# One transformer-style layer on one core: tokens spread over the partitions by a product, setup reordered, eight products of ones on TensorE

## What is computed

```
w_emb = fake_quant(emb_weight)                 # scale = max|w| / 127, round, scale back
e = w_emb[tok]                                 # 125 x 128 table, tokens 0..124
h = relu(conv over the previous and this token, fake_quant(conv_weight))
x = layernorm(h)
Wq = w_qkv / sigma_est * sigma                 # sigma_est by one power step: v = W u, u2 = W^T v
q, k, v = split(x @ Wq.T);  dots = q k^T * exp(temperature), own position masked
h = h + softmax(dots) v @ Wo.T + b_out         # Wo scaled in the same way
h = h + experts(layernorm(h))
```

## Time and profile before

| | |
|---|---|
| median of 3 runs | 495.35 us (495.01 to 495.76) |
| profiled execution, its own time | 495.01 us |
| its span, first to last instruction | 493.2 us |
| outside the span | 1.8 us |
| TensorE busy | 472.3 us (96% of the span), 3824 instructions |
| VectorE busy | 423.6 us (86%) |
| ScalarE busy | 363.8 us (74%) |
| GpSimd busy | 300.6 us (61%) |

### The profile page before, as it was taken

How to read it: one execution, slowest core, us unless ns; L and a number is a source line. 1 busy time by engine, 2 the same in 40 slices (tenths; PEclk the granted TensorE clock), 3 DMA queues, 4 the chain that set the end, 5 groups by cost and what they waited for, 6 DMA issues and landing times.

```text
span 493.2 us, 11360 instructions
## 1 busy us (share of the span) xinstructions
PE 472.3 (96%) x3824; PEld 404.6 (82%) x3824; DVE 423.6 (86%) x722; ACT 363.8 (74%) x688; POOL 300.6 (61%) x357
## 2 busy tenths in 40 slices
PE   2989999999999999999999999999999999999897
PEld 2945788888988898888788898889888988888685
DVE  5469989988998898889998999899989999999465
ACT  1258878887788778877888688878887887683553
POOL 2114697888668866874468857885788556751000
DMA  6500009531953195362622592259225932000002
GB/s 233 218 1 0 2 15 213 127 87 36 200 116 85 34 200 120 85 131 52 126 66 68 108 202 59 73 105 204 56 72 105 202 69 64 0 2 3 3 17 73
DMA packets 29484, 44.78 MB, mean 91 GB/s; under 512 B 3200, under 2 KB 21120, under 8 KB 29184
## 3 DMA queue, kind: packets, MB, share of 16 engines
q1 hardware_dynamic: 28864, 44.21, 38.4%
q10 hardware_dynamic: 576, 0.00, 0.1%
HBM read 6.46 MB, written 1.05 MB: 15 GB/s over the span
## 4 chain that ended last, share of the span: by engine, by line
PE 81%; DVE 13%; issue 2%; DMA 2%; ACT 2%; SPq 0%; POOL 0%; DVEq 0%; ACTq 0%
PE ps L696 22%; PE ps L680 19%; PE ps L662 10%; PE ps L663 10%; PE ps L603 5%; DVE pt_lo L1361 4%; DVE neg_max L1377 4%; PE ps L739 3%; PE ps L598 2%; PE ps L887 2%; DMA arena<-in_wqkv_rows 2%; PE ps L870 2%; PE ps L573 1%; DVE x L1198 1%; PE ps L901 1%
## 5 line engine op out<-in xcount | busy, mean ns | idle before, releaser
L1361 DVE TENSOR_TENSOR pt_lo<-ps,pt_hi 128x512 fp32r<-128x512 f32 x256 | 163.5, 680 | 1.3 <-ACT pt_hi L1036 1.3
L1377 DVE TENSOR_REDUCE neg_max<-ps 128x1 f32<-128x1024 f32 x128 | 156.6, 1223 | 6.5 <-PE ps L667 2.6
L1036 ACT ACTIVATE pt_hi<-ps 128x512 fp32r<-128x512 f32 x256 | 139.3, 596 | 29.4 <-PE ps L680 29.2
L438 POOL TENSOR_SCALAR probs<-probs,inv_sum 128x1024 f32<-128x1024 f32 x128 | 144.6, 1129 | 26.6 <-POOL inv_sum L435 26.6
L696 PE MATMUL ps<-pt_hi,v_slot 128*128 128x256 f32 x512 | 150.0, 324 | 0.0
L1056 ACT ACTIVATE probs<-ps,neg_max 128x1024 f32<-128x1024 f32 x128 | 142.5, 1113 | 6.9 <-DVE neg_max L1377 4.0
L680 PE MATMUL ps<-ident,probs 128*128 128x128 f32 x1024 | 133.7, 273 | 1.5 <-DVE pt_lo L1361 0.9
L680 PEld LDWEIGHTS ps<-ident,probs 128*128 128x128 f32 x1024 | 117.6, 140 | 19.8 <-POOL probs L438 3.0
L696 PE MATMUL ps<-pt_lo,v_slot 128*128 128x256 f32 x512 | 127.8, 282 | 0.0
L435 POOL TENSOR_TENSOR inv_sum<-row_sum,powers 128x1 f32<-128x1 f32 x128 | 70.8, 553 | 83.2 <-ACT probs L1056 83.2
L696 PEld LDWEIGHTS ps<-pt_hi,v_slot 128*128 128x128 f32 x512 | 96.8, 189 | 9.7 <-issue 9.7
(11 more groups left out here) (145 smaller groups left out, 391.6 us busy)
## 6 DMA issues: line engine op xcount, KB each, us to landing
q_st<-arena SPq DMA_DIRECT2D x28, 256.0 KB, 3.8
k_hi<-arena SPq DMA_DIRECT2D x28, 256.0 KB, 5.1
k_lo<-arena SPq DMA_DIRECT2D x28, 256.0 KB, 5.2
v_slot<-v_all SPq DMA_DIRECT2D x14, 512.0 KB, 3.9
arena<-arena SPq DMA_DIRECT2D x28, 256.0 KB, 4.9
f_sb<-in_f SPq DMA_DIRECT2D x2, 1024.0 KB, 10.1
x<-in_tok SPq DMA_DIRECT2D x2, 512.0 KB, 7.6
w_slot<-in_w_pairs SPq DMA_DIRECT2D x8, 128.0 KB, 2.0
```

What stands on the lines that cost most here:

```text
L438: pool.tensor_scalar(probs[:, t % 4, :], probs[:, t % 4, :], inv_sum[:, t % 4:t % 4 + 1], 1.0, ALU.mult, ALU.mult).then_inc(norm_done, 1)
L1036: act.activation(dst, ps[:, transposes_bank(t, a, drain), :].rearrange("p (j c) -> p j c", c=P), ACT.Copy).then_inc(hi_done, 1)
L1361: dve.tensor_tensor(pt_lo[at], ps[:, transposes_bank(t, a, drain), :].rearrange("p (j c) -> p j c", c=P), pt_hi[at].bitcast(F32), ALU.subt ...
L1377: dve.tensor_reduce(neg_max[:, t % 4:t % 4 + 1], ps[:, SCORES + 2 * (t % 2):SCORES + 2 * (t % 2) + 2, :].rearrange("p a c -> p (a c)"), AX ...
```

## The change

It touches only the setup and the first step of the first pair.

- The tokens are loaded once, as 16 rows of 128 (8 KB). GpSimd caps them and converts them (`tok_f`), then `tokens_apart(b)` multiplies, for eight rows, the row by a column of `ident`, so that each of 16 partitions holds 1024 elements with its own 128 tokens at its own place and zeros elsewhere. TensorE's `spread_tokens(b)` multiplies this with a matrix of ones of 16 rows: two products of 512 columns, after which every partition of the bank holds the tokens. VectorE compares out of PSUM, in two halves.
- `conv` and the tokens are issued by ScalarE, ahead of `u_sb`; the weight rows are second in SyncE's queue.
- GpSimd makes five constants first (`ident` first of all), then does tokens and the four steps of the convolution's quantisation, then the other constants.
- TensorE runs eight products of `ones` with itself, which nobody reads, between `spread_tokens(0)` and the wait for the weight rows. The Gram matrix is cut in four products before the embedding and eight after `embed(1)`. The order is now: `top`, spread 0, ones, Gram 0 to 3, `embed(0)`, spread 1, `embed(1)`, Gram 4 to 11, `embed(2)`, `gu`, transposes.
- `v_ps` moves behind the projection `dq0`; the first head's order is `dk0`, `dq0`, `dk1`, `dq1`, in other banks; the ratio stands ahead of the first `first_low`.
- `embed(3)` moves behind the first scores, into step 0 of the first pair, with ScalarE's `embedded(3)` and then the exponential of step 0 ahead of that step's values.

```diff
-        top, gram_ps, gu_ps, sums_ps = ps[:, 2, 0:VOCAB], ps[:, 3, 0:P], ps[:, 3, 0:1], ps[:, 3, 0:2]
-        v_ps, u2_ps, out_sums_ps = ps[:, TRANS, 0:1], ps[:, PV_BANK, 0:4], ps[:, WORK, 0:2]
+        top, gram_ps, gu_ps = ps[:, 2, 0:VOCAB], ps[:, 3, 0:P], ps[:, 3, 0:1]
+        sums_ps, v_ps, u2_ps, out_sums_ps = ps[:, WORK, 0:2], ps[:, WORK, 4:5], ps[:, WORK, 8:12], ps[:, WORK, 0:2]
...
-        EMBED_BANKS = (0, 1, 2, WORK)
-        FIRST_HEAD = {"dk0": WORK, "dk1": TRANS, "dq0": 2, "dq1": TRANS + 1}
+        TOKEN_BANKS = TRANS
+        EMBED_BANKS = (0, 1, 2, TRANS)
+        FIRST_HEAD = {"dk0": 0, "dq0": 1, "dk1": 3, "dq1": TRANS + 1}
...
+            const(pool.memset(ident[:, :], 0.0))
+            pool.wait_ge(const_ready, count[0])
+            const(pool.affine_select(out=ident[:, :], in_=ident[:, :], compare_op=ALU.not_equal, fill=1.0,
+                                     base=0, pattern=[[-1, P]], channel_multiplier=1))
             const(pool.memset(ones[:, :], 1.0))
+            const(pool.memset(ones_r[:, :].bitcast(F32), 1.0))
...
+            pool.wait_ge(tok_loaded, 16)
+            pool.tensor_scalar(tok_f[:, :], tok_sb[:, :], float(VOCAB - 1), 1.0, ALU.min, ALU.mult).then_inc(tok_ready, 1)
+            pool.wait_ge(const_ready, 2)
+            pool.wait_ge(tok_ready, 1)
+            def tokens_apart(b):
+
+                pool.tensor_tensor(tok_diag[:, b, :, :], tok_f[:, :].unsqueeze(1).broadcast_to([TILES, NT, P]),
+                                   ident[0:TILES, NT * b:NT * (b + 1)].unsqueeze(2).broadcast_to([TILES, NT, P]),
+                                   ALU.mult).then_inc(tok_ready, 1)
+
+            tokens_apart(0)
+            conv_flat = conv_sb[0:VOCAB, :, :].rearrange("p k d -> p (k d)")
+            conv_q = quant[0:VOCAB, D:3 * D]
+            pool.wait_ge(setup_dve, SETUP_CONV)
+            pool.tensor_scalar(conv_q, conv_flat, qs[0:VOCAB, 6:7], ROUND, ALU.mult, ALU.add).then_inc(conv_steps, 1)
+            pool.wait_ge(conv_steps, 1)
+            pool.tensor_scalar(conv_q, conv_q, ROUND, qs[0:VOCAB, 4:5], ALU.subtract, ALU.mult).then_inc(conv_steps, 1)
+            pool.wait_ge(conv_steps, 2)
+            pool.tensor_tensor(conv_q, conv_q, conv_flat, ALU.subtract).then_inc(conv_steps, 1)
+            pool.wait_ge(conv_steps, 3)
+            pool.tensor_tensor(conv_q, conv_flat, conv_q, ALU.add).then_inc(conv_steps, 1)
+
+            tokens_apart(1)
...
-            tokens(0)
             sp.dma_start(wr_sb, wqkv_rows).then_inc(rows_loaded, 16)
-            tokens(1)
...
+            def spread_tokens(b):
+
+                pe.wait_ge(tok_ready, b + 2)
+                for c in range(2):
+                    pe.matmul(ps[:, TOKEN_BANKS + 2 * b + c, :], ones_r[:, :],
+                              tok_diag[:, b, 4 * c:4 * c + 4, :], start=True, stop=True).then_inc(tok_mm, 1)
...
+            spread_tokens(0)
+            for _ in range(8):
+                pe.matmul(ps[:, 1, 0:P], ones[:, :], ones[:, :], start=True, stop=True)
             pe.wait_ge(rows_loaded, 16)
-            for t in range(12):
-                last = pe.matmul(gram_ps, wr_sb[:, t, :], wr_sb[:, t, :], start=t == 0, stop=t == 11)
-            last.then_inc(setup_pe, 1)
-
+            gram(0, 4)
+            pe.wait_ge(setup_dve, SETUP_TABLES)
+            pe.wait_ge(one_hot_ready, 2)
+            embed(0).then_inc(h_mm, 1)
+            spread_tokens(1)
+            pe.wait_ge(one_hot_ready, 3)
+            embed(1).then_inc(h_mm, 1)
+            gram(4, 12).then_inc(setup_pe, 1)
+            pe.wait_ge(one_hot_ready, 5)
+            embed(2).then_inc(h_mm, 1)
             pe.wait_ge(u_loaded, 16)
             pe.wait_ge(setup_act, 2)
             pe.matmul(gu_ps, gram_sb, u_sb[:, 0:1], start=True, stop=True).then_inc(setup_pe, 1)
...
+            transpose_rows(0)
+            transpose_rows(1)
...
+                if kind == "dq0":
+                    pe.wait_ge(wout_loaded, 32)
+                    pe.wait_ge(setup_dve, SETUP_RATIO)
+                    for j in range(H // 2):
+                        last = pe.matmul(v_ps, wo_sb[:, j, :], u_sb[:, 1 + j:2 + j], start=j == 0, stop=j == H // 2 - 1)
+                    last.then_inc(setup_pe, 1)
...
+                if pair.i == 0 and (k, t) == (0, 0):
+                    embed(3).then_inc(h_mm, 1)
                 if fresh and t < 4:
                     first_values(t)
...
+            act.dma_start(conv_sb[:, :, :].rearrange("p k d -> p (k d)"),
+                          conv.rearrange("(o k) d -> o (k d)", o=1).partition_broadcast(P)).then_inc(conv_loaded, 16)
+            act.dma_start(tok_sb[:, :], tok.rearrange("b (t n) -> (b t) n", n=P)).then_inc(tok_loaded, 16)
             act.dma_start(u_sb[:, :], u_cols).then_inc(u_loaded, 16)
...
                         if first:
+                            if t == 0:
+                                embedded(3)
+                                exponentials(pair, k, t)
                             first_values(t)
-                            exponentials(pair, k, t)
+                            if t > 0:
+                                exponentials(pair, k, t)
...
-                dve.tensor_scalar(one_hot[b][:, 1:SEQ + 1], tok_sb[b], float(VOCAB - 1), vocab_id[:, :],
-                                  ALU.min, ALU.is_equal).then_inc(one_hot_ready, 1)
...
+                for c in range(2):
+                    dve.wait_ge(tok_mm, 2 * b + c + 1)
+                    dve.tensor_scalar(one_hot[b][:, 1 + HALF * c:1 + HALF * (c + 1)], ps[:, TOKEN_BANKS + 2 * b + c, :],
+                                      vocab_id[:, :], None, ALU.is_equal).then_inc(one_hot_ready, 1)
+
+            rows_of(0)
+            dve.wait_ge(conv_steps, 4)
...
                 variances(g)
+                if g == 0:
+                    rows_of(1)
```

More of the change, by code:

```diff
@@ L155, in layer_kernel @@
         const_ready = sem("const_ready")
-        tok_loaded = [sem(f"tok_loaded{b}") for b in range(B)]
+        tok_loaded = sem("tok_loaded")
+        tok_ready = sem("tok_ready")
+        tok_mm = sem("tok_mm")
+        conv_steps = sem("conv_steps")
         emb_loaded = sem("emb_loaded")
@@ L564, in embed, with gram, transpose_rows @@
                 return ins
-            pe.wait_ge(const_ready, N_CONST)
+            def spread_tokens(b):
[3 more added lines that the diff above has]
+                              tok_diag[:, b, 4 * c:4 * c + 4, :], start=True, stop=True).then_inc(tok_mm, 1)
+            def gram(first, end):
+                for t in range(first, end):
+                    last = pe.matmul(gram_ps, wr_sb[:, t, :], wr_sb[:, t, :], start=t == 0, stop=t == 11)
+                return last
+            def transpose_rows(c):
+                for t in range(4 * c, 4 * c + 4):
+                    pe.wait_ge(xhat_done, t + 1)
+                    ins = pe.transpose(ps[:, 5 + c, t % 4 * P:(t % 4 + 1) * P], x_hat[0][:, t, :], ident[:, :])
+                ins.then_inc(xt_mm, 1)
+            pe.wait_ge(const_ready, N_FIRST_CONST)
             pe.wait_ge(setup_dve, SETUP_DIAG)
             pe.matmul(top, ones[0:VOCAB, :], quant[0:VOCAB, 0:VOCAB], start=True, stop=True).then_inc(setup_pe, 1)
+            spread_tokens(0)
+            for _ in range(8):
+                pe.matmul(ps[:, 1, 0:P], ones[:, :], ones[:, :], start=True, stop=True)
             pe.wait_ge(rows_loaded, 16)
-            for t in range(12):
-                last = pe.matmul(gram_ps, wr_sb[:, t, :], wr_sb[:, t, :], start=t == 0, stop=t == 11)
-            last.then_inc(setup_pe, 1)
+            gram(0, 4)
[8 more added lines that the diff above has]
+            embed(2).then_inc(h_mm, 1)
             pe.wait_ge(u_loaded, 16)
@@ L578, in _ @@
             pe.matmul(gu_ps, gram_sb, u_sb[:, 0:1], start=True, stop=True).then_inc(setup_pe, 1)
-            pe.wait_ge(setup_dve, SETUP_TABLES)
-            for c in range(4):
-                if c % 2 == 0:
-                    pe.wait_ge(one_hot_ready, c + 2)
-                embed(c).then_inc(h_mm, 1)
-            pe.wait_ge(wout_loaded, 32)
-            for j in range(H // 2):
-                last = pe.matmul(v_ps, wo_sb[:, j, :], u_sb[:, 1 + j:2 + j], start=j == 0, stop=j == H // 2 - 1)
-            last.then_inc(setup_pe, 1)
-            for t in range(NT):
-                pe.wait_ge(xhat_done, t + 1)
-                ins = pe.transpose(ps[:, 5 + t // 4, (t % 4) * P:(t % 4 + 1) * P], x_hat[0][:, t, :], ident[:, :])
-                if t % 4 == 3:
-                    ins.then_inc(xt_mm, 1)
+            transpose_rows(0)
+            transpose_rows(1)
             def project_values(t, bank):
@@ L988, in _ @@
                 high_twice(kind, 0, bank).then_inc(first_hi, 1)
+                if kind == "dq0":
+                    act.wait_ge(setup_pe, 5)
+                    act.activation(norm_sb[:, 12:13], v_ps, ACT.Copy).then_inc(setup_act, 1)
             act.wait_ge(setup_pe, 6)
@@ L1181, in _ @@
```

(5 more changed lines are left out.)

71 lines of the change are left out of this document (35 added, 36 removed).

## The result

| | before | after |
|---|---|---|
| median of 20 executions each, taken in turns | 495.59 us | 498.17 us |
| ratio, 95% interval | 1 | 1.0056 (1.0033 to 1.008) |
| start of the table products on VectorE | 10.87 | 13.10 |
| E, start of `embed(0)` | 15.59 | 15.44 |
| S, first scores | 30.67 | 30.84 |

A forecast was written before the change was run, and what follows sets the result against it. TensorE's order in the setup was taken as the bound, then VectorE's first steps. First scores 3.67 us earlier, less 2.27 given back in step 0, gave 1.4 us gained: 493.9 us, range 492.2 to 496.2.

The forecast's parts named there:

- E of the changed kernel: Setup: after spread, ones and Gram 0 to 3, `embed(0)` starts at 12.4 us, against 15.73 before.
- Tokens: ScalarE's transfer queue: the small token transfer lands right behind the convolution's rows, at 4.5 us.
- Rival E: Setup transfers: tokens stuck behind the convolution land at 6.5, `embed(0)` starts at 14.4, loss 0.6 us, 495.9; chance 0.12.
- GpSimd: Setup: cap, `tokens_apart(0)` (2.4) and waits take 2.95 us ahead of the spread; the convolution's four steps take 2.9.
- Tables: VectorE, setup: the two table products take 0.7 us behind GpSimd's convolution steps.
- The other condition of `embed(0)`: Setup: the table that `embed(0)` also needs is ready at 11.05 us, ahead of TensorE.
- TensorE's stretch: Setup, spread from 7.45 to Gram's end at 12.4: spread 0.85 us, ones to 11.5, eight Gram passes 0.9.
- The point at which the pace changes: TensorE, setup: passes quicken from 0.213 to 0.112 us 3.8 us after the busy stretch starts, at 11.25.
- Rival D: TensorE's pace changes later than 3.8 us after the spread's start: gain 0.4 or loss 1.2 us; chance 0.15.
- E to S: From start of `embed(0)` to first scores: 14.6 us, against 14.94 before, putting first scores at 27.0.
- Step 0: First step of the first pair: `embed(3)` and ScalarE's new order give back 2.27 us.
- Rival F: Tokens land at 8.8 like those of before; ones wholly on the path, loss 2.9 us, 498.2; chance 0.10.

The follow-up runs named there:

- run 8: Changed kernel with the tokens first on ScalarE's queue and the convolution behind `emb` on SyncE's; 499.6 us, 1.006 of the kernel before.
- run 2: Changed kernel with `tokens_apart(1)` waiting until VectorE has made the tables; 497.72 us, 1.003 of the kernel before.
- run 1: The changed kernel measured again without any edit, as control; 501.18 us, 1.0078 of the kernel before.
- run 6: Changed kernel with `embed(3)` back behind `embed(2)` and ScalarE's old order in step 0; 497.69 us, 1.005 of the kernel before.
- run 7: Changed kernel with only ScalarE's exponential of step 0 back behind the values; 497.79 us, 1.0054 of the kernel before.
- run 5: Kernel before with only `embed(3)`, `embedded(3)` and the exponential placed in step 0 as in the change; 497.88 us, 1.007 of the kernel before.
- run 9: Kernel before plus an unused GpSimd operation of the form of `tokens_apart` beside VectorE's rounding of the taps; 495.66 us, one execution.
- run 3: Changed kernel without the eight products of ones; 500.35 us, 1.0088 of the kernel before.
- run 10: Changed kernel with the convolution back on SyncE's queue, `tokens_apart(1)` behind the tables and `embed(3)` back in the setup; 493.58 us, 0.9969 of the kernel before.
- run 11: Run 10 with taps rounded on VectorE, all twelve Gram products ahead of `embed(0)`, three ones, `gu` and largest tap moved; 492.73 us, 0.9955 of the kernel before.
- run 4: Changed kernel without the products of ones and with `tokens_apart(1)` behind the tables; 499.29 us, 1.0052 of the kernel before.

## Why the prediction was wrong

The forecast was 493.9 us (gain 1.4); 498.17 was measured, above the range. What failed is the step "E of the changed kernel": 12.4 was predicted, 15.44 came. What led up to it, term by term:

- **Tokens.** "I take them right behind it", 4.5. They landed 2.2 later, at 6.7. The step took the convolution's 3.6 us from the earlier trace rows, where it stood second behind `emb` with no other small transfer beside it; at the head of the second queue it takes 5.0 and holds up what stands with it. Run 8 shows that the order is the cause of the tokens' lateness, though not of the convolution's 5.0: there it takes 5.1 in its old place. Rival E's place (6.5) was nearly right, its price (a loss of 0.6) wasn't.
- **GpSimd.** From the tokens' landing to the spread, or to the end of `tokens_apart(0)`, 2.95 predicted and 2.9 measured (6.7 to 9.57; the operation itself 1.89, not 2.4, the rest waits and the cap). The four steps of the convolution 2.9 predicted, 3.45 measured (9.61 to 13.06): L405, with the scalar from memory in second place, takes 1.15 where L403 of the same size takes 0.58.
- **Tables.** 0.7 predicted, 2.29 measured. This is the term that no rival had: `tokens_apart(1)`, right behind the steps on GpSimd's queue, holds the first table product. "The other condition of `embed(0)`" came at 15.4 instead of 11.05: 2.2 by the tokens, 0.55 by the steps, 1.6 by the hold. The sum had given it 1.35 us of cover against TensorE's 12.4. The tokens take nothing from this cover, since both conditions follow from them; the steps and the hold, 2.15 together, used it up, though TensorE's own stretch grew by 0.6.
- **TensorE's stretch.** From the start of the spread to the end of Gram 4.95 was predicted (7.45 to 12.4), 5.6 measured (9.57 to 15.15): the spread took 1.15 instead of 0.85 and the ones 3.54 instead of 3.2, to the next start each. For the 0.85 the prediction had no row: the passes of the earlier trace rows that it names take 0.44 each at the fast pace, which would be 1.77 for two at half of it. Without the tables E would have been at about 15.2, where rival E's arithmetic with tokens at 6.5 gives 14.4. In run 2 the tables are out of the way; there the pace changed within Gram, and E was at 15.35.
- **The point at which the pace changes.** 3.8 us behind the start was one row's reading (by the starts of the passes it is 4.0). In four profiles with the same program up to E it came 4.6 (after), 6.9 (run 1), 3.9 (run 6) and 7.0 (run 7) behind the start of the spread; in the kernel before and in runs 5 and 9 4.0, 4.7 and 6.0 behind the start of Gram. It is not a constant that a sum can use. Rival D came true on top of E: in the profile after with the ones slow, in runs 1 and 7 with Gram slow throughout too.

**Right:** the ones bring up the pace of what follows and are worth their time (runs 1 and 3: 1.6 us of R, 1.2 by the last column), and the wait for the weight rows is gone. **E to S** was 15.4 against 14.6: the first two embeddings and the spread between them took 4.7 instead of 4.1, and from the copy of `xt` (24.39) to the scores it was 6.45 against 6.1. **Step 0** gave back 1.98 (runs 5 and 6: 2.01 each) against 2.27.

So the sum reads: S predicted 3.67 earlier, measured 0.17 later, of which E 3.0 and E to S 0.8; step 0 costs 2.0; R is 0.17 + 1.98 = 2.15 later. The rest of the medians' 2.6 us is not pinned down; one part that the profiles show is the pace, which changed early in the profile after and has E 0.4 and 0.6 later in runs 1 and 7. **Rival F**'s time, 498.2, is what was measured, but its cause, tokens at 8.8, isn't: they landed at 6.7. A right number from a wrong cause is not a hit. The point from which it decides, tokens after 5.9, was passed, so the sign follows from the prediction's own arithmetic once the landing is known.

Which edit is the loss? In the measured runs the placement of the two small transfers is the largest single piece (run 8: 2.2 us of R against the profile after, 2.8 by the last column). `tokens_apart(1)` ahead of the tables is worth 0.2 (run 2) while the tokens are late, because TensorE comes to E hardly earlier. With the tokens early the hold binds alone: in run 8 the table products start at 10.88 and TensorE idles 1.21 ahead of E at 13.22; in run 10, with the hold gone and `embed(3)` back (0.2, run 6), E is at 11.43 and R 2.0 earlier again. I haven't run the change with the hold alone taken out beside the new order of transfers, so how the 2.0 is divided between these two rests on run 6's 0.2.

## What to carry to other kernels

Before work goes to GpSimd because it is idle, look at what VectorE does in the same microseconds: here a large two-input operation of GpSimd held VectorE's wide operations on SBUF until it ended, so put it beside VectorE's reads of PSUM or behind the last operation that somebody waits for. Put the smallest transfer that heads a chain first in its queue: here that brought its landing from 6.7 to 2.6 us. When two chains meet at one point, a term that both share moves both and leaves the cover between them as it was; what uses it up is what each has alone, here 0.55 and 1.6 us against a cover of 1.35. And before a chain in one profile is called the bound, look at a second execution: here the two conditions of `embed(0)` changed places.

## What the runs showed of the hardware

**The hold.** A wide operation of VectorE on SBUF that starts beside a large two-input operation of GpSimd ends with it: 1.86 instead of 0.29 (L1216 after), 1.96 instead of 0.29 (first table product), 1.86 instead of 0.35 (run 9), and one that had started already runs through (L1161, 0.35). It is not so for every operation on SBUF. Small ones pass: in run 11 a scale and a reciprocal of 125x1 take 0.15 and 0.16 as ever at 4.95 and 5.14, beside `tokens_apart(0)` (3.62 to 5.51). In the profile after eight aggregations of 128x6 pass beside a two-input operation, while the 128x8 addition behind them, which takes 0.17 for 128x4 elsewhere, is held to its end; VectorE first, then GpSimd:

```profile
60.12 0.64 DVE L1254 BATCH_NORM_AGGREGATE mv<-stats 128x2 f32<-128x6 f32 x8
60.79 0.63 DVE L1257 TENSOR_SCALAR rstd<-mv 128x8 f32<-128x8 f32 x1
```

```profile
60.11 1.28 POOL L464 TENSOR_TENSOR arena<-arena 128x512 fp32r<-128x512 f32 x1 [0.18 <-POOL arena L462]
```

A two-input operation of GpSimd of only 128x4 did not hold either: in run 10 three normalisations of 128x128 take their 0.34 beside it (L432, 18.24 to 19.28). A compare out of PSUM isn't held: in run 8 L1236 takes 0.74 at 10.16, as alone, beside the two-input L409 (10.12 to 10.84). One-input operations of GpSimd do little (L1217 in run 2, beside L403: 0.53, usually 0.29). And where VectorE begins first, GpSimd is the one that is lengthened: in run 8 VectorE's L1218 starts at 9.16 and takes its 0.29, L407 of GpSimd starts 2 ns behind it and takes 0.88 instead of 0.73; in run 9 the operation that starts behind L1161 takes 2.05 instead of 1.89. A row of the kernel before shows it too, and I had passed over it, VectorE first, then GpSimd:

```profile
67.97 0.98 DVE L1198 TENSOR_SCALAR x<-h_sb,mv,rstd 128x128 f32<-128x128 f32 x2
```

```profile
67.31 1.30 POOL L428 TENSOR_TENSOR arena<-arena 128x512 fp32r<-128x512 f32 x1 [0.18 <-POOL arena L426]
```

Two normalisations that take 0.34 each otherwise take 0.98 and end 0.3 us behind the GpSimd addition. The Trainium skill ("GPSIMD Engine Reference", section "Specifications") says that GpSimd shares its SBUF interfaces with VectorE and contends with VectorE's instructions that have two SBUF inputs or run in a two-port mode. The trace agrees: the table product has two such inputs. The rounding has one; "VectorE: DVE Perf Modes" (section "Mode 2×_2P — use both read ports for one tensor") says that a tensor-scalar operation on SBUF may use both read ports, which would make it one of these. That the hold lasts to the end of the GpSimd operation is what the runs show.

**The start of the transfers.** The same 8 KB took 5.5 us behind the repeated convolution and 1.8 at the head of its queue; the 64 KB of the embedding, on the other queue, 3.6 when the repeated convolution was issued with it and 2.0 when it was not. The convolution itself took 3.6 before and 5.0 to 5.1 after, in either place.

**The pace and the clock's column.** In all stretches of the setup the column of the granted clock reads 1.00, at 9 to 13 instructions in 2 us as at 18 to 20. The trace itself says more: its record of the granted clock begins, at full clock, at 14.22 after, 16.25 in run 1, 13.48 in run 6, 16.62 in run 7, 19.67 in run 3 and 22.56 in run 4, each time where the spacing of the passes falls from 0.213 to 0.112; for the time ahead of its first entry the column counts 1.00, and in the kernel before there is no entry at all. So a 1.00 early in a span is no sign of the fast pace, and the spacing of the passes is. Late in the span the column does show a fall, to 0.50, in some executions and at one place.
